# Causal attention scores: one key-major form for all blocks, float32r operands in two row halves, masks on GpSimd

## What is computed

```python
Q = (content @ Wq).reshape(b, n, HEADS, HEAD_DIM)   # K, V alike; HEADS = 16, HEAD_DIM = 16
scores = jnp.einsum('bqhd,bkhd->bhqk', Q, K) / math.sqrt(HEAD_DIM)
alpha = jax.nn.softmax(scores, axis=-1)
causal = jnp.tril(jnp.ones((n, n), dtype=bool))
alpha = jnp.where(causal, alpha, jnp.zeros((), dtype=alpha.dtype))
Y = jnp.einsum('bhqk,bkhd->bqhd', alpha, V).reshape(b, n, d)
x = _layernorm(x + Y, axis=-1)
```

## Time and profile before

| | |
|---|---|
| time of three runs | 1908.29, 1912.72 (median), 1913.53 us |
| span of the profiled execution | 1938.8 us |
| instructions | 31529 |
| PE, PEld, DVE, ACT, POOL busy | 86%, 53%, 59%, 65%, 13% of the span |
| stage 1 | 0 to some 102 us |
| attention | first score matmul at 119.7 us, last at 1093.8 us |
| routing and experts | from there to the end |

### The profile page before, as it was taken

How to read it: one execution, slowest core, us unless ns; L and a number is a source line. 1 busy time by engine, 2 the same in 40 slices (tenths; PEclk the granted TensorE clock), 3 DMA queues, 4 the chain that set the end, 5 groups by cost and what they waited for, 6 DMA issues and landing times. The chain is left out here.

```text
span 1938.8 us, 31529 instructions
## 1 busy us (share of the span) xinstructions
PE 1658.6 (86%) x10758; PEld 1025.6 (53%) x10759; DVE 1151.0 (59%) x2219; ACT 1268.4 (65%) x1416; POOL 251.4 (13%) x251
## 2 busy tenths in 40 slices
PE   7848999999999999999999742099999999999990
PEld 6623433333333333334333442078988988889880
DVE  6855767768677676676877642045354444554533
ACT  7748999999999999999999710024233333332422
POOL 0000000000000000000000033612111221131111
PEclk9969999999999999999999855589999999999995
DMA  5577010100101101011010121333131412322016
GB/s 174 175 206 234 17 33 16 33 26 23 33 16 33 28 22 33 18 31 30 20 33 16 40 98 50 105 121 89 35 101 16 115 52 67 105 65 63 12 12 183
DMA packets 91081, 124.92 MB, mean 64 GB/s; under 512 B 10240, under 2 KB 76544, under 8 KB 91008
## 3 DMA queue, kind: packets, MB, share of 16 engines
q1 hardware_dynamic: 76416, 106.85, 17.4%
q0 software_dynamic: 14592, 17.06, 4.8%
HBM read 74.78 MB, written 51.18 MB: 65 GB/s over the span
## 5 line engine op out<-in xcount | busy, mean ns | idle before, releaser
L697 ACT ACTIVATE probs<-scores 128x1536 f32<-128x1536 f32 (+1 forms) x384 | 520.6, 1379 | 48.7 <-PE scores L627 43.5
L627 PE MATMUL scores<-aq,ak 98*128 98x512 bf16 (+3 forms) x1280 | 304.1, 352 | 61.5 <-DMA aq<-shift_dram 26.8
L740 DVE TENSOR_REDUCE sums<-expq 128x1 f32<-128x1408 f32 (+6 forms) x448 | 347.3, 827 | 13.8 <-ACT expq L703 13.8
L643 PE MATMUL o_ps<-probs,vh 128*32 128x512 f32 (+3 forms) x2560 | 340.0, 543 | 0.0
L1386 ACT ACTIVATE gate<-up_ps 128x512 f32<-128x512 f32 x128 | 76.5, 598 | 350.8 <-PE up_ps L1278 348.6
L627 PE MATMUL scores<-ak,aq 98*128 98x512 bf16 (+3 forms) x1184 | 264.5, 343 | 17.0 <-ACT probs L697 9.0
L703 ACT ACTIVATE expq<-scores 128x1536 f32<-128x1536 f32 x192 | 274.8, 1449 | 2.0
L627 PEld LDWEIGHTS scores<-aq,ak 98*128 98x128 bf16 x1280 | 96.8, 98 | 235.4 <-ACT probs L697 72.8
L627 PEld LDWEIGHTS scores<-ak,aq 98*128 98x128 bf16 x1184 | 91.2, 98 | 238.5 <-ACT expq L703 94.7
L727 DVE TENSOR_TENSOR hidden<-probs,after 128x384 f32<-128x384 f32 x128 | 70.9, 554 | 243.9 <-ACT probs L697 243.9
L1278 PE MATMUL up_ps<-xeT_hi,wup_hi 128*128 128x512 f32 x512 | 205.7, 402 | 11.4 <-issue 9.9
(11 more groups left out here) (209 smaller groups left out, 2378.8 us busy)
## 6 DMA issues: line engine op xcount, KB each, us to landing
raw<-w_T SPq DMA_DIRECT2D x16, 1024.0 KB, 10.0
split_dram<-parts SPq DMA_DIRECT2D x48, 256.0 KB, 2.9
aq<-split_dram SPq DMA_DIRECT2D x192, 64.0 KB
xe_dram<-blank SPq DMA_DIRECT2D x1, 10560.0 KB, 56.1
raw<-wg_T SPq DMA_DIRECT2D x8, 1024.0 KB, 8.7
xin<-xe_dram SPq DMA_DIRECT2D x8, 792.0 KB, 5.5
ak<-split_dram SPq DMA_DIRECT2D x32, 192.0 KB
xin<-xe_dram SPq DMA_DIRECT2D x8, 528.0 KB, 3.8
```

Source lines behind the costliest of these rows:

```text
L627: last = nc.tensor.matmul(dst[:, at:at + w], still, moving[0:KS, lo:lo + w], start=True, stop=True, skip_group_check=True)
L643: last = nc.tensor.matmul(dst[32 * r:32 * r + 32, BLK - w:BLK], vh[j % 2][:, k, :], probs[:, m % P_RING, at:at + w], start=first, stop=Tru ...
L697: last = nc.scalar.activation(probs[:, m % P_RING, 0:w], src[:, 0:w], ACT.Exp, scale=HD ** -0.5)
L740: last = nc.vector.tensor_reduce(sums[:, j % 2, col:col + 1], expq[:, n % X_RING, at:at + w], AX.X, ALU.add)
```

## The change

Every score block becomes key-major: 64 blocks of 128 keys by 512 queries per head, packed by three in 22 tiles, the last with one block. All go to `probs`. `ORDER`, `expq`, the accumulator, DVE's sums and both mask tables are gone. Q and K are kept in two float32r parts, so three products of parts and one row for the shift make 49 rows; the operands are held twice, from partition 0 and from partition 64, and blocks take the copies in turn. The row of constants that multiplies the shift is made once and sent to the operands by four transfers.

```diff
-ORDER = "KQKKKQKQKQQKQKQKKKQQKQ"
+BLOCKS = [(g, k) for g in range(NG) for k in list(range(4 * g, 4 * g + 4)) + [k for k in range(NT) if k // 4 != g]]
+NBK = len(BLOCKS)
+NS = -(-NBK // SPAN)
+NU = NBK // 4
...
+UNIT_AT = {}
+for u in range(NU):
+    UNIT_AT.setdefault(tile_of(4 * u + 3) + S_RING, []).append(u)
+TURN_AT = {tile_of(16 * g + 15) + S_RING + 1: g for g in range(NG)}
...
-            parts = sb(st, "parts", [P, 3, U, N], BF16)
-            rest = sb(st, "rest", [P, 2, BLK])
+            parts = sb(st, "parts", [P, 2, U, N], FP32R)
...
-                    for u in range(U + 1):
+                    for u in range(U):
...
-                        if u >= 1:
-                            act.wait_ge(proj_read, at + U)
-                            nc.scalar.activation(parts[:, 1, u - 1, cols], rest[:, (u - 1) % 2, :], ACT.Copy).then_inc(mid_ready, 1)
...
-                            nc.vector.tensor_tensor(rest[:, u % 2, :], proj[:, u, :], hi[u], ALU.subtract).then_inc(proj_read, 1)
-                        if u >= 1:
-                            dve.wait_ge(mid_ready, at)
-                            nc.vector.tensor_tensor(lo[u - 1], rest[:, (u - 1) % 2, :], mid[u - 1], ALU.subtract).then_inc(proj_split, 1)
+                        nc.vector.tensor_tensor(parts[:, 1, u, cols], proj[:, u, :], parts[:, 0, u, cols].bitcast(FP32), ALU.subtract).then_inc(proj_split, 1)
...
+        KR = 3 * HD
+        KS = KR + 1
+        HALVES = (0, P // 2)
+        AQ = (0, 1, 0)
+        AK = (0, 0, 1)
...
+            for at in range(3):
+                rows = slice(row + at * HD, row + (at + 1) * HD)
+                sp.dma_start(aq[j][rows, :].bitcast(FP32), split_dram[0, AQ[at], bass.ds(n * HD, HD), :]).then_inc(done, 16)
+                sp.dma_start(ak[j][rows, :].bitcast(FP32), split_dram[1, AK[at], bass.ds(n * HD, HD), :]).then_inc(done, 16)
...
+                    for row in HALVES:
+                        load_operands(sp, j, n, row, a_loaded[j])
+                        sp.dma_start(aq[j][row + KR:row + KS, :].bitcast(FP32), shift_dram[bass.ds(n, 1), :]).then_inc(a_loaded[j], 16)
...
+                def mask(i, j, g):
+
+                    pool.wait_ge(exp_done, i * (2 * NS) + (j * NS + tile_of(16 * g + 3) + 1 + S_RING))
+                    pool.wait_ge(pv_done, i * (2 * NU) + (j * NU + NU + 4 * g - 8 + 3))
+                    pool.sem_inc(masking, 1)
+                    for r in range(4):
+                        nc.gpsimd.affine_select(out=seen[:, g % 2, r, :], in_=slot(j, 16 * g + r)(P * r, P * (r + 1)), compare_op=ALU.is_ge, fill=0.0,
+                                                base=0, pattern=[[1, P]], channel_multiplier=-1).then_inc(mask_done, 1)
...
+                    for n in range(SPAN * t, min(SPAN * t + SPAN, NBK)):
+                        (g, k), row, at = BLOCKS[n], HALVES[n % 2], n % SPAN * BLK
+                        last = nc.tensor.matmul(scores[t % S_RING][:, at:at + BLK], ak[j][row:row + KS, k * P:(k + 1) * P],
+                                                aq[j][row:row + KS, g * BLK:(g + 1) * BLK], start=True, stop=True, skip_group_check=True)
+                    last.then_inc(scores_ready, 1)
...
+                        for n in range(4 * u, 4 * u + 4):
+                            k = BLOCKS[n][1]
+                            r = k % 4
+                            last = nc.tensor.matmul(o_ps[g % O_RING][32 * r:32 * r + 32, :], vh[j % 2][:, k, :] if k < 4 * g else only_sum[:],
+                                                    slot(j % 2, n)(0, BLK), start=False, stop=True, skip_group_check=True)
...
+                            if before_it >= 0 and masks_in(before_it):
+                                act.wait_ge(mask_done, i * (8 * NG) + (j * (4 * NG) + masks_in(before_it)))
+                            w = width_of(t)
+                            nc.scalar.activation(probs[:, (j * NS + t) % P_RING, 0:w], scores[t % S_RING][:, 0:w], ACT.Exp, scale=HD ** -0.5).then_inc(exp_done, 1)
```

More of the change, by code:

```diff
@@ L75 @@
-KT = key_tiles()
-QT = query_tiles()
-NK, NQ = len(KT), len(QT)
-ORDER = "KQKKKQKQKQQKQKQKKKQQKQ"
-assert ORDER.count("K") == NK and ORDER.count("Q") == NQ
-MANY = [n for n in range(NQ) if len(QT[n]) > 1]
-Q_ORDER = MANY + [n for n in range(NQ) if n not in MANY]
-SEQ = []
-for c in ORDER:
-    n = sum(1 for k, _ in SEQ if k == c)
-    SEQ.append((c, n if c == "K" else Q_ORDER[n]))
-NS = len(SEQ)
-NM = len(MANY)
-K_POS = [n for n, (k, _) in enumerate(SEQ) if k == "K"]
-Q_POS = {m: n for n, (k, m) in enumerate(SEQ) if k == "Q"}
@@ L124 @@
-UNITS = product_units()
-AFTER = [[(back, work, what[t + back * NS]) for back in (1, 0) for work, what in (("unit", UNIT_AT), ("turn", TURN_AT)) if t + back * NS in what]
-         for t in range(NS)]
-DVE_ORDER = ((0, "mask", 0), (1, "take", 3), (0, "sum", 0), (0, "take", 0), (1, "gather", 3), (1, "final", 0),
-             (0, "mask", 1), (0, "gather", 0), (0, "sum", 1), (0, "sum", 2), (0, "sum", 3), (0, "take", 1),
-             (0, "sum", 4), (0, "mask", 2), (0, "sum", 5), (0, "gather", 1), (0, "take", 2), (0, "mask", 3),
-             (0, "gather", 2))
+SPAN = 3
@@ L565, in _ @@
                 sp.wait_ge(x_loaded, 16)
+                sp.wait_ge(minus_stored, 64)
             @block.gpsimd
@@ new lines, in masked, with products @@
+                def masked(j, g):
+                    for r in range(4):
+                        nc.tensor.matmul(o_ps[g % O_RING][32 * r:32 * r + HD, P * r:P * (r + 1)], vh[j][:, 4 * g + r, 0:HD], seen[:, g % 2, r, :],
+                                         start=False, stop=True, skip_group_check=True)
+                def products(i, j, u):
+                    g = u // 4
+                    if u % 4 == 0:
+                        pe.wait_ge(out_read, i * (2 * NG) + (j * NG + g + 1))
+                        last = diagonal(j % 2, g)
+                    else:
+                        if u % 4 == 2:
+                            pe.wait_ge(mask_done, i * (8 * NG) + (j * (4 * NG) + 4 * g + 4))
+                            masked(j % 2, g)
+                        for n in range(4 * u, 4 * u + 4):
[3 more added lines that the diff above has]
+                                                    slot(j % 2, n)(0, BLK), start=False, stop=True, skip_group_check=True)
+                    last.then_inc(pv_done, 1)
@@ L661, in turn, with behind @@
                     last.then_inc(out_turned, 1)
+                def behind(i, j, t, older, newer):
+                    for back in (1, 0):
+                        if (older and back) or (newer and not back):
+                            for u in UNIT_AT.get(t + back * NS, ()):
+                                products(i, j - back, u)
+                            if t + back * NS in TURN_AT:
+                                turn(i, j - back, TURN_AT[t + back * NS])
                 def head(i, j, older):
-                    pe.wait_ge(a_loaded[j], i * (16 * (A_DMAS + 1)) + 16 * (A_DMAS + 1))
+                    pe.wait_ge(a_loaded[j], i * (16 * LOADS) + 16 * LOADS)
                     pe.wait_ge(vh_ready, i * 2 + (j + 1))
@@ L668, in head @@
                         fill(i, j, t)
-                        for back, work, which in AFTER[t]:
-                            if older or not back:
-                                (products if work == "unit" else turn)(i, j - back, which)
+                        behind(i, j, t, older, True)
                 head(0, 0, False)
@@ L677, in _ @@
                         head(i, j, True)
+                pe.wait_ge(exp_done, pairs * (2 * NS) + S_RING)
                 for t in range(NS):
-                    for back, work, which in AFTER[t]:
-                        if back:
-                            (products if work == "unit" else turn)(pairs, -back, which)
+                    behind(pairs, 0, t, True, False)
             @block.scalar
```

327 lines of the change are left out of this document (105 added, 222 removed).

## The result

| | before | changed |
|---|---|---|
| median of the timed runs | 1911.55 us (1908.29 to 1913.53, 4 runs) | 2035.78 us (2030.61 to 2038.47, 4 runs) |
| ratio | | 1.0636, 95% interval 1.061 to 1.0662 |
| span of the profiled execution | 1938.8 us | 2032.3 us |
| first exponential of attention | 121.1 us | 130.1 us |
| from the first to the last exponential | 973.1 us | 1089.4 us |

The change is 6.4% slower. The forecast had 81 us more, it became 124. The traces divide it: 9.1 us until the first exponential and 116.3 us in attention, together 125. What lies behind attention lasts from 810 to 855 us in the profiles of this case; on one chip the kernels lie 7 to 15 us apart there. The profile before is 27 us longer than the timed runs of the same kernel, 845 us of it behind attention, against 813 in the changed kernel's.

A forecast was written before the change was run, and what follows sets the result against it. ACT was taken to bound attention at 30.19 us a head, with PE taking over at 32.8. The sum +83 - 4 - 2 + 6 - 2 = +81 us gave 1994 us, 80% range 1925 to 2070.

The forecast's parts named there:

- PE takes over the pace: Attention, per head: PE needs 32.6 us against ACT's 28.6, so PE replaces ACT as the pace; chance 0.67.
- Prices of PE: Attention, per head: PE's fills 13.3 us, product units 17.1 and transposes 2.2, 32.6 us together.
- Two fills on end: Attention score fills: one ahead of another fill costs 0.55 us, one behind another fill 0.54 us, four of each.
- ACT still makes it wait a little where two fills follow each other; I take 0.2: Attention, per head: PE's waits for ACT add 0.2 us to its 32.6, giving 32.8 us.
- The start: Ahead of attention: norms -4 us, shift subtraction -2, more transfers before the first fill +6 (3 to 10).
- the -2: Head 2's 5.17 us wait for its load behind the clearing store shrinks by about 2 us as heads get slower.
- No pairing: Rival, attention fills: float32r matmuls in the two halves go one after another; 37.4 us a head, 2142 us; chance 0.10.
- Loads ahead: Rival, attention fills: weight loads run under the products ahead, saving 0.11 us in 18 fills; 1940 us; chance 0.10.
- ACT as pace: Rival, attention: PE needs about 29 us or less, ACT decides at 29.7 us a head; 1895 us; chance 0.13.
- The estimate by the Trainium skill: Attention fills: a pair of blocks in two halves takes 0.30 us instead of 0.23, a head 34.3 us.
- GpSimd and DMA hidden: Attention, per head: GpSimd's 16 selections (4.6 us) and 14 load transfers (about 7 us to issue) delay nothing.

The follow-up runs named there:

- The run with the constant rows first: The changed kernel with the four constant-row transfers issued after the first head's loads and ahead of the second head's; 2053.9 us, 1.059 times the kernel before.
- the run with short units: The changed kernel, constant rows sent early, with six product units above the diagonal taking 64 columns instead of 512; 2106.7 us, 1.0867 times the kernel before.
- the mixed kernel with 49 rows in two halves: The kernel before, its tiles, DVE sums and masks kept, with float32r operands in two row halves and constant rows sent early; 1966.9 us, ratio 1.013.
- the mixed kernel with one half: Tiles, DVE sums and masks of the kernel before, float32r operands, all fill matmuls in the lower row half; 2510.0 us, 1.2947 times the kernel before.
- the one with wide selections: The changed kernel, constant rows sent early, with each GpSimd selection over 512 columns instead of 128; 2023.7 us, 1.06 times the kernel before.

## Why the prediction was right, and where its sum was off

The direction, the new pace and the range held; the median lies 42 us above the forecast.

- **PE takes over the pace: right.** ACT back to back would need 28.6 us of the 33.95; in mid-stage it waits 3.9 us a head for scores from PE.
- **Prices of PE: right where they had a row.** Fill ahead of products 0.65 forecast, 0.66 measured; second start in the same half 0.34 and 0.334; plain unit 1.00 and 0.996; masked 1.24 and 1.20; transposes 0.55 and 0.585; diagonal 1.03 and 0.996. The text speaks of four matmuls of line 647; they are three, six instructions, and the period drawn from them stands.
- **Two fills on end: too dear.** 0.55 + 0.54 forecast, 0.89 measured. The six blocks alternate between the halves across the tile's edge and make three couples; I had counted two couples and two single blocks. That is 0.8 us a head, and with the small differences above it brings PE's own work from 32.6 to 31.5.
- **"ACT still makes it wait a little where two fills follow each other; I take 0.2": this step failed.** The place was right, since 2.0 of the 2.4 us lie in pairs of fills or right behind them; the size wasn't, and the 0.3 us at the transposes had no term. The waits are 2.4 us a head, +70 us over 32 heads, of which the cheaper fills give back 35. The mean of PE lay 4 us above ACT's, and I took that distance for room. It is one only on average: a tile with a fill alone costs PE 0.45 to 0.66 and ACT 1.34, one with a masked unit costs PE 1.86. The runs line up with this: waits 0.2 with 37.4 us of own work, 0.7 with 34.3, 2.4 with 31.5, 2.8 with 29.9. The nearer PE comes to ACT, the more of what is saved is given back. That the uneven tiles are the cause is argued from the timelines; the one run that changed the order alone left the waits at 2.4. Forecast 32.6 + 0.2, measured 31.5 + 2.4: two errors of opposite sign hid in an error of 1.1 us a head, +37 us.
- **The start: direction right, size off.** Stage 1 gave more than forecast (its blocks had been 10.3 us apart, 72 us over seven intervals, not 10.2): the last norms stand at 87 us, 6 before, for the 4 I had taken, and the subtraction of 2.3 us is gone. SP's loads begin at 97.6 and all is issued at 112.2, earlier than I had it. But I took the landing as shorter than before's 8.6 us and it was 16.6: first fill at 128.8 for "118 to 122", 9.1 us later than before. The run with the constant rows first shows it to be their place in the queue.
- **The first heads: -4 us for the -2.** The first three take 106.6 us in place of 99.4 us, 7 more, where three times 3.76 would be 11. The first is long in itself, 38.7 us: after 36.8 idle us PE runs at the clock's lower level for 14 us (128 to 142), before for 8 (119 to 127).
- **Sum as measured:** 32 x 3.76 = 120, -4, +9: 125 us.
- **Rivals.** No pairing: excluded, its price confirmed. Loads ahead: not seen, at every change of shape the first load starts with its matmul, as in the earlier trace rows; the rule of the Trainium skill (TensorE: Matmul & The Clock Gate, Part 2) on weight loads pulled ahead doesn't show across these changes. Its condition is row groups that don't conflict, and the products in flight take all 128 rows, so this case doesn't test it. ACT as pace: no, though own work is 1.1 us nearer to it than I had summed.
- **The estimate by the Trainium skill** (TensorE: Matmul & The Clock Gate, Part 3: 3.07x for four row tiles), 0.30 us for a pair: here the second block of a pair costs nothing, 0.66 against 0.89, so its 34.3 us a head was met only by chance, out of waits.
- **GpSimd and DMA hidden: right**, the first tested at double length. No wait for operands stands in mid-stage.

## What to carry to other kernels

When an edit makes another engine the pace, don't compare means: write the two engines' costs tile by tile, with the number of buffers between them, and sum the later of the two. What lies between ACT's 28.6 and PE's 31.5 was no free room but 2.4 us of waits, and each saving on PE gave less than its price. A few small transfers issued last can hold a whole stage; put what the first instruction needs ahead of what the second head needs. And look at the granted clock of every run before reading its time: the run with short units priced nothing because it had fallen.

## What the hardware showed that I hadn't expected

In kernels with float32r matmuls of 49 rows PE lost its clock while it was busy for 92 to 98% of the time, with no gap above 0.8 us in mid-stage where the clock was full. In mid-stage (260 to 1060 us) the mean granted clock was 1.00 in before, in the change and its variants with all product work, and with bf16 operands even when the product work was cut; it was 0.94 and 0.95 in the mixed kernel with 49 rows in two halves, 0.87 in the change with short units, and 0.63 in the mixed kernel with one half. Filling the rows up to 64 with zeros, which changes neither the result nor the time of a fill, held it at 1.00. What exactly the chip looks at stays open: whether the zeros would do the same for the short units, whether it is the rows or the use of both halves in full, wasn't tried. Whether short gaps must come with the low rows is open as well: the change itself has 49 rows and held its clock with PE busy for 97%, and with one half and 100%. With 49 rows two levers moved it, the product work beside the fills and the halves in use.

The attention stage of a kernel repeats within 1 us from chip to chip (1089.4, 1088.8 and 1089.0 us for the change and two variants with its order), while what follows it took 845 us in the variant with the constant rows first and 810 us in the one with wide selections, on another chip. Ratios on one chip and stages of the trace are safe; spans from different chips aren't.
